# The first expert group's weight splits in another order: down weights first, the next group's weights last

## What is computed

```python
x2 = rmsnorm(hid, ln2_w).reshape(-1, h)
probs = jax.nn.softmax(x2 @ gate_w.T, axis=-1)
top_w, top_i = jax.lax.top_k(probs, TOPK)            # 4 of 16
top_w = top_w / jnp.sum(top_w, axis=-1, keepdims=True)
wfull = jnp.sum(jax.nn.one_hot(top_i, E) * top_w[..., None], axis=1)
gu = jnp.einsum('th,eih->tei', x2, w1)
g, u = (gu[..., :I], gu[..., I:])                    # I = 176
down = jnp.einsum('tei,ehi->teh', jax.nn.silu(g) * u, w2)
routed = jnp.einsum('te,teh->th', wfull, down)
sgu = x2 @ sh_gu_w.T
sg, su = (sgu[..., :SHI], sgu[..., SHI:])            # SHI = 352
shared = jax.nn.silu(sg) * su @ sh_down_w.T
return hid + (routed + shared).reshape(b, s, h)
```

## Time and profile before

| what | us |
|---|---|
| median of 3 runs | 776.35 (775.97 to 777.61) |
| profiled execution, its own time | 777.51 |
| its span | 775.4 |
| PE busy | 735.3 (95%) |
| DVE busy | 570.8 (74%) |
| ACT busy | 458.2 (59%) |
| GpSimd busy | 345.0 (44%) |

### The profile page before, as it was taken

How to read it: one execution, slowest core, us unless ns; L and a number is a source line. 1 busy time by engine, 2 the same in 40 slices (tenths; PEclk the granted TensorE clock), 3 DMA queues, 4 the chain that set the end, 5 groups by cost and what they waited for, 6 DMA issues and landing times.

```text
span 775.4 us, 12318 instructions
## 1 busy us (share of the span) xinstructions
PE 735.3 (95%) x4036; PEld 573.7 (74%) x4036; DVE 570.8 (74%) x1222; ACT 458.2 (59%) x1022; POOL 345.0 (44%) x305
## 2 busy tenths in 40 slices
PE   7997899999989999999999999998998999999996
PEld 3443455455555888998999889888777888888986
DVE  3699999998898678848875775786674555647376
ACT  4699868868674467637654773665662433425153
POOL 1007989998779644415342432232432221313130
PEclk9998999999999999999999999999999999999999
DMA  8022433444222100100100101002239251516101
GB/s 327 13 75 82 120 98 110 121 109 103 74 84 70 53 28 28 45 11 29 56 28 3 51 27 28 22 21 64 81 81 235 74 165 47 149 49 180 47 0 55
DMA packets 25212, 59.02 MB, mean 76 GB/s; under 512 B 3616, under 2 KB 5152, under 8 KB 25040
## 3 DMA queue, kind: packets, MB, share of 16 engines
q1 hardware_dynamic: 25024, 58.21, 25.7%
q10 hardware_dynamic: 144, 0.26, 0.1%
HBM read 57.21 MB, written 1.25 MB: 75 GB/s over the span
## 4 chain that ended last, share of the span: by engine, by line
PE 48%; issue 18%; DVE 15%; POOL 11%; ACT 5%; DMA 1%; DVEq 0%; SPq 0%; POOLq 0%; ACTq 0%
PE ps L1036 10%; PE ps L1038 9%; PE ps L1037 9%; PE ps L551 8%; POOL a_p L1163 4%; POOL m_ring L408 3%; DVE m_ring L905 3%; POOL a_wl L1157 2%; PE ps L500 2%; PE ps L456 2%; PE ps L509 2%; DVE e_aw L2072 2%; PE ps L1226 2%; PE ps L555 2%; DVE e_sg L2064 1%
## 5 line engine op out<-in xcount | busy, mean ns | idle before, releaser
L1163 POOL TENSOR_TENSOR a_p<-a_p,a_rs 128x128 f32<-128x128 f32 x124 | 58.9, 506 | 166.4 <-DVE a_rs L1494 166.4
L1733 POOL TENSOR_TENSOR e_wl<-raw,e_wh 128x512 fp32r<-128x512 f32 (+1 forms) x55 | 59.1, 1085 | 155.0 <-ACT e_wh L1869 86.4
L551 PE MATMUL ps<-m_ring,ident 128*128 128x512 f32 x256 | 121.3, 602 | 5.5 <-POOL m_ring L408 5.3
L408 POOL TENSOR_TENSOR m_ring<-m_ring,m_c_sb 128x1024 f32<-128x1024 f32 x40 | 94.6, 2373 | 15.3 <-DVE m_ring L905 13.7
L400 POOL TENSOR_TENSOR m_ring<-m_du,m_b_sb 128x1024 f32<-128x1024 f32 x31 | 73.7, 2376 | 59.1 <-DVE m_ring L892 59.1
L551 PEld LDWEIGHTS ps<-m_ring,ident 128*128 128x128 f32 x256 | 46.9, 191 | 50.2 <-issue 37.5
L1383 ACT ACTIVATE a_p<-a_p,a_nmax 128x128 f32<-128x128 f32 (+1 forms) x128 | 57.0, 447 | 37.3 <-DVE a_nmax L1487 37.1
L1036 PE MATMUL ps<-a_rowsh,e_wh 128*128 128x512 f32 x200 | 78.3, 391 | 0.2 <-ACT e_sg L1914 0.2
L1037 PE MATMUL ps<-a_rowsl,e_wh 128*128 128x512 f32 x200 | 77.9, 389 | 0.0
L1038 PE MATMUL ps<-a_rowsh,e_wl 128*128 128x512 f32 x200 | 77.8, 389 | 0.0
L905 DVE TENSOR_TENSOR_SCAN m_ring<-m_first,ps 128x1024 f32<-128x1024 f32 x32 | 72.8, 2275 | 6.6 <-ACT ps L754 4.5
(11 more groups left out here) (233 smaller groups left out, 2119.9 us busy)
## 6 DMA issues: line engine op xcount, KB each, us to landing
raw<-in_expert_w SPq DMA_DIRECT2D x30, 384.0 KB, 3.4
raw<-in_attn_w SPq DMA_DIRECT2D x20, 512.0 KB, 3.4
m_c_sb<-bc SPq DMA_DIRECT2D x40, 256.0 KB, 3.5
m_b_sb<-bc SPq DMA_DIRECT2D x32, 256.0 KB, 4.2
e_wb<-wt SPq DMA_DIRECT2D x18, 256.0 KB, 4.6
e_wb<-wt SPq DMA_DIRECT2D x4, 448.0 KB, 6.4
e_wb<-wt SPq DMA_DIRECT2D x4, 384.0 KB, 4.4
x<-in_x_tok SPq DMA_DIRECT2D x1, 1024.0 KB, 10.0
```

The costliest lines, as they stand in the source:

```text
L408: nc.gpsimd.tensor_tensor(split(slot(n)), split(slot(n)), c_sb[:, k % C_BUFS:k % C_BUFS + 1, :].to_broadcast([P, 2, HALF]), ALU.mult).then ...
L551: nc.tensor.matmul(ps[:, Y_BANK + c, :], ident[:, :], slot(n)[:, c * HALF:(c + 1) * HALF], start=False, stop=False, skip_group_check=True) ...
L1163: nc.gpsimd.tensor_tensor(p[:, b, cols], p[:, b, cols], rs[:, b, t:t + 1].to_broadcast([P, count]), ALU.mult).then_inc(norm_done, 1)
L1733: nc.gpsimd.tensor_tensor(w[1][:, k, cols], raw[:, k, cols], w[0][:, k, cols].bitcast(F32), ALU.subtract).then_inc(low, 1)
```

## The change

On GpSimd group 0 leaves the loop: first all five low parts of the down weights, then all five of group 1's gate and up weights. ACT does the five down casts in `late_weights`, behind the activations of block 2, and group 1's five gate and up casts behind those of block 4. DVE adds down tile 0 ahead of low part 9. PE's and SP's instructions stay as they are.

```diff
@@ -1740,7 +1740,11 @@
         for i in range(TT):
             nc.gpsimd.tensor_tensor(hid[:, i, :], hid[:, i, :], x1[:, i, :], ALU.add).then_inc(x_added, 1)
         rest(4, 4, slice(0, 2 * D), wh_done, w_done)
-        with pool.Fori(0, NMG) as g:
+        for k in range(GM):
+            rest(k, k, slice(2 * D, 3 * D), dh_done, d_done)
+        for k in range(GM):
+            rest(GM + k, k, slice(0, 2 * D), wh_done, w_done)
+        with pool.Fori(1, NMG) as g:
             for k in range(GM):
                 for kd in DOWN_AT[k]:
                     rest(g * GM + kd, kd, slice(2 * D, 3 * D), dh_done, d_done)
@@ -1939,9 +1943,8 @@
         def late_weights():
 
             act.wait_ge(wf_done, 1)
-            for k in range(2):
+            for k in range(GM):
                 high_d(0, k)
-                high_w(k, 32)
 
         def take_weights():
             act.wait_ge(wT_ready, 1)
@@ -1962,13 +1965,18 @@
                     take_weights()
                     high(n + 1, 1, k, 1)
                     late_weights()
-                for kd in DOWN_AT[k]:
-                    high_d(g, kd)
+                if not first:
+                    for kd in DOWN_AT[k]:
+                        high_d(g, kd)
                 if not (first and k == 2):
                     if k < GM - 1:
                         high(n, 0, k, 0)
                     high(n + 1, 1, k, 1)
-                high_w(k, g * 16 + 32)
+                if not first:
+                    high_w(k, g * 16 + 32)
+            if first:
+                for k in range(GM):
+                    high_w(k, 32)
 
         group(0)
         with act.Fori(1, NMG) as g:
@@ -2115,6 +2123,9 @@
                 products(g, n + 1, 1, k, 1)
                 if k < GM - 1:
                     low(n, 0, k, 0)
+                if first and k == GM - 1:
+                    dve.wait_ge(x_added, TT)
+                    add_down(g, 0)
                 low(n + 1, 1, k, 1)
 
         mean_squares(0)
@@ -2128,8 +2139,7 @@
         mean_squares(1)
         scale_rows(1)
         tiles(0)
-        dve.wait_ge(x_added, TT)
-        for i in range(TT):
+        for i in range(1, TT):
             add_down(0, i)
         with dve.Fori(1, NMG - 1) as g:
             tiles(g)
```

## The result

The changed kernel takes 772.84 us (median of 12 runs, 771.93 to 776.31) against 777.60 for the kernel before (775.86 to 783.36 in the same sessions): a ratio of 0.9934, 95% interval 0.9917 to 0.9951, so 3.8 to 6.5 us less. The forecast was 771.6 in a range of 769.9 to 774.2. The profiled execution took 772.44 us.

A forecast was written before the change was run, and what follows sets the result against it. PE, otherwise full, was held by four waits in group 0, the longest 2.08 us on DVE's addition. 3.9 us of waits plus 1.6 of clock made 5.5, 777.51 to 772.0 profiled; median forecast 771.6, range 769.9 to 774.2.

The forecast's parts named there:

- The stretching: Group 0's experts: GpSimd's work lengthens DVE instructions with two SBUF operands; 2.77 us of this would leave.
- The addition: DVE's queue in group 0: adding down sum 0 ahead of low part 9 is alone worth 1.4 us.
- the sum's 3.9 us: PE in group 0: down tile 2 starts at 586.9, 3.9 us sooner, before any clock gain.
- The wait left: PE before down tile 2 of group 0: one wait of some 0.5 us on DVE's addition remains.
- The load for group 2: SP's weight loads, now sent from 588.9: the first lands by 598.7, ACT needs it at 602.0; costs nothing, up to 0.5.
- Rival (c): Group 2's first weights land too late, stalling ACT and PE; 778 if landing took 20 us; chance 0.04 with other slowdowns.
- The lock: DVE's low part 9 might wait up to 1.28 us for GpSimd's shared ports; 0 in the sum, 0.9 in the range.
- the clock's: PE's granted clock, low from 592 to 596 behind the waits, stays full in group 0's down products; 1.6 us gained.
- (a): PE's low clock stays or comes elsewhere; 772.4 at best, 774 if a second stretch appears; chance 0.15.
- (b): DVE's long instructions in group 0 aren't GpSimd's doing; only reordering counts, 1.4 us, giving 775.0; chance 0.05.
- (d): ACT's casts for down weights 3 and 4 would wait for loads; chance 0.04, shared with a gain under 1.5 us.

The follow-up runs named there:

- the idle subtractions: Changed kernel plus four unneeded GpSimd subtractions in SBUF behind its five down low parts; ratio 0.9973 to the kernel before.
- memsets: Changed kernel plus ten unneeded GpSimd memsets, which write SBUF and read nothing, behind the down low parts; ratio 0.9940 to the kernel before.
- the changed kernel, again: The changed kernel with nothing edited, run once more on the experiments' first chip; 774.67 us against 779.16 for the kernel before, ratio 0.9948.

## Why the prediction was right

The steps in its own order, with 0.81 us added to its times for the later start:

- ACT: the first Silu at 577.1; it started at 577.05. PE's wait on it is gone.
- GpSimd: down low parts done by 579.7 to 580.0; done at 579.73. PE's wait is gone.
- DVE: low part 8 at 585.9 and product 9 at 587.2; they ended at 585.72 and 587.05. The stretching was GpSimd's, as the idle subtractions show. Its size was put at 2.77 us; the four durations shrank by 2.56 (the two low parts took 1.48 with ACT's cast between them, not the 1.30 that I had counted), and low part 8 ended 2.75 us sooner from the common point.
- The addition: 1.4 us alone; 1.4 measured (D1 15.57 to 14.17). Low part 9 behind it wasn't missed by tile 4.
- PE: tile 2 at 586.9 + 0.81 = 587.7, measured 587.70; the sum's 3.9 us were 3.87. The wait left was 0.23 and not 0.5. DVE was ready 0.18 us before PE had finished down sum 0, so that the addition now waits for PE and no longer for DVE's own queue.
- The load for group 2: issued at 589.64 and landed 3.5 us later, against the 9.8 that I took as the worst, and ACT used it at 602.83. Rival (c) had 9.7 us of room and not 3.3.

```profile
raw<-in_expert_w SPq DMA_DIRECT2D x1, 384.0 KB, 3.5
```

- The lock: low part 9 started at 587.75, ahead of GpSimd's first long low part at 588.32, so it cost nothing, and the additions, with an operand in PSUM, kept 0.42 us while GpSimd worked. The Trainium skill (SBUF — State Buffer, "SBUF: two separate sides") says that a VectorE instruction with two SBUF inputs contends with a GpSimd instruction that reads SBUF and not with one that only writes it. The runs agree: up to 1.59 us beside subtractions, 0.69 beside memsets.

One term was mis-sized, the clock's. I booked 1.6 us as lost in the kernel before and regained. In the two profiled executions it was 1.64, since one had the fall and the other hadn't. The second profile of the kernel before shows that it isn't in every execution. So the sure gain is D1's 3.87 us, and the clock adds 1.6 in the executions that had it. I did leave this open for the median, between 770.85 and 772.45; the measured 772.84 lies just beyond the upper of these. But the median of the kernel before was itself 777.60 over 12 runs, not 776.35: the difference of the medians is 4.8, between 3.9 and 5.5. The forecast gain was 4.75 us (776.35 to 771.6) and the measured one 4.76; agreement this close is luck, since the interval runs from 3.8 to 6.5. In how many of the timed runs the clock fell can't be told from the times, because something larger moves them (below).

The upper end of the range was added up wrongly: (a) at 772.4 with 0.9 and 0.5 is 773.8 and not 774.2. The measured time lies inside either way.

Of the rivals, (a) didn't come about in either profile of the changed kernel, and in the kernels with one part of the change undone it came only with ACT's old order (a wait of 2.42 us) and GpSimd's (11.38). (b) is ruled out by the idle subtractions, (d) by the timelines: the casts for down weights 3 and 4 waited for nothing.

## What to carry to other kernels

Where VectorE's instructions with two SBUF operands are longer than the same form elsewhere, look at what GpSimd reads at that time, before looking at who waits for GpSimd: here the visible wait on it was 0.48 us, its effect through VectorE 2.75. Moving GpSimd's work out of such a stretch needs the engine that feeds it to change its order as well; here GpSimd's half without ScalarE's gained nothing (0.9989, and 1.2 us of D1 worse than the addition alone), and ScalarE's half without GpSimd's cost 1.2%. And in an in-order queue put the instruction that frees a PSUM bank ahead of one whose result is needed two tiles later, above all where the latter waits for another engine anyway.

## What the runs showed of the hardware that was not expected

- The granted clock fell behind waits of 0.48, 0.65 and 2.08 us in one execution, and not in another with the same waits to 0.05 us.
- PE took the down products of a group behind its gap in 14.38 or in 14.75 us, at a granted clock of 1.00. In one and the same execution (the changed kernel, again) groups 1 and 2 took 14.75 and group 3 took 14.38. The cause is open; it is worth up to 1.5 us over four groups. The 0.32 us behind the stretch fit it: group 1 took 14.76 us in the profile of before and 14.37 in that of the changed kernel.
- Executions of one kernel differ by more than the change gives, and some of that begins at one instruction in the Mamba scan. GpSimd's first down low part started between 574.51 and 576.00 us in eleven profiles and at 579.17, 579.50 and 579.64 in three. In just these three a VectorE instruction of four columns at 214 us, L932, took 2.39 or 2.40 us, where it took 0.15 or 0.16 in the eleven others. It starts within 0.03 us of a GpSimd product of 2.4 us, and which of the two the trace puts first doesn't tell the outcome: GpSimd's stands 0.01 us ahead in one of the three and in two of the eleven. The kernel before, VectorE's and GpSimd's timelines, first the profile of the earlier trace rows, then the second:

```profile
213.90 0.16 DVE L932 TENSOR_SCALAR norm<-stats 128x4 f32<-128x4 f32 x1
...
213.91 2.36 POOL L400 TENSOR_TENSOR m_ring<-m_du,m_b_sb 128x1024 f32<-128x1024 f32 x1
```

```profile
214.80 2.40 DVE L932 TENSOR_SCALAR norm<-stats 128x4 f32<-128x4 f32 x1
...
214.81 2.36 POOL L400 TENSOR_TENSOR m_ring<-m_du,m_b_sb 128x1024 f32<-128x1024 f32 x1
```

From this instruction to its second occurrence 47.2 us pass in the three, 43.5 in eight others and 45.0 in the other three; from there to the common point it is 316.1 to 317.9 in all fourteen. So the late executions lose 2.2 to 3.7 us here, and the times of the kernel before spread over 7.5. That this is the same effect as in the experts is likely but not shown, since L932 has one SBUF input and not two. One with two, L941 of eight columns, stands a little later beside another such GpSimd product and took 2.27 to 2.29 us in all fourteen profiles, against 0.17 at its second occurrence. No run here moved either instruction, so what doing so would gain isn't known.
